# A softmax's division moved from the probabilities to the head's output

## What is computed

```python
q = (layernorm(x) @ wq)          # 32 heads of 128, rotary; scaled by 1/sqrt(128)
k, v = ctx @ wk, ctx @ wv        # 8 heads of 128 over 1024 positions; each serves 4 query heads
attn = softmax(q @ k.T + mask)   # per batch element and head: 512 x 1024
out = attn @ v                   # 512 x 128 per head
x = x + concat(out) @ wo
```

## Time and profile before

| | |
|---|---|
| median of 3 runs | 3843.18 us |
| the runs | 3857.33, 3840.72, 3843.18 us |
| span of the profiled execution (first to last instruction) | 3848.1 us |
| the profiled execution's own time | not listed apart from the runs |
| attention stage in the trace | about 1250 to 2218 us |
| mean granted TensorE clock | 0.905 |

### The profile page before, as it was taken

One profiled execution on the slowest core, in us unless ns is written; L12 is line 12 of the kernel. 1 busy time (PEld: TensorE's weight loads), 2 busy tenths in 40 slices (PEclk: granted clock), 3 DMA queues, 4 the chain that ended last, 5 costly groups with the idle time before them and its releaser, 6 DMA issues. The chain is left out here.

```text
span 3848.1 us, 45676 instructions
## 1 busy us (share of the span) xinstructions
PE 3119.9 (81%) x14144; PEld 2487.0 (65%) x14144; DVE 3251.7 (85%) x4335; ACT 2177.6 (57%) x2742; POOL 1180.3 (31%) x547
## 2 busy tenths in 40 slices
PE   5767665767766999999999977777574699999999
PEld 4555554546645788888888855555442577777787
DVE  7999997877977899999999979999947488878853
ACT  4555554546556677777777655666513265555531
POOL 3777774741732111111111135545100001101000
PEclk8888886889878999999999989989856799999999
DMA  3222223324222211111111032222002212121211
GB/s 107 79 93 71 98 71 103 105 89 142 87 90 93 89 53 52 57 52 54 56 47 58 28 137 98 96 89 87 22 6 88 66 61 77 60 82 61 71 55 52
DMA packets 170336, 286.81 MB, mean 75 GB/s; under 512 B 11712, under 2 KB 98752, under 8 KB 170176
## 3 DMA queue, kind: packets, MB, share of 16 engines
q1 hardware_dynamic: 160960, 268.24, 20.9%
q10 hardware_dynamic: 9216, 16.78, 1.2%
HBM read 196.64 MB, written 88.34 MB: 74 GB/s over the span
## 5 line engine op out<-in xcount | busy, mean ns | idle before, releaser
L220 DVE SCALAR_TENSOR_TENSOR pq_nf_val<-pq_nf_above,pq_nf_val 128x1024 f32<-128x1024 f32 x224 | 449.3, 2006 | 10.2
L898 ACT ACTIVATE at_pth<-at_t 128x512 fp32r<-128x512 f32 x512 | 281.9, 596 | 249.5 <-PE at_t L991 249.5
L205 ACT ACTIVATE pq_nf_above<-pq_nf_raw,sharp 128x1024 f32<-128x1024 f32 x240 | 273.7, 1148 | 256.6 <-DVE pq_nf_val L220 255.1
L220 DVE SCALAR_TENSOR_TENSOR ou_nf_val<-ou_nf_above,ou_nf_val 128x1024 f32<-128x1024 f32 x224 | 395.1, 1764 | 5.8
L205 ACT ACTIVATE ou_nf_above<-ou_nf_raw,sharp 128x1024 f32<-128x1024 f32 x240 | 274.6, 1150 | 197.9 <-DVE ou_nf_val L220 184.3
L117 PE MATMUL pq_pj<-xT_h,pq_wh 128*128 128x512 f32 x512 | 227.4, 444 | 180.1 <-POOL pq_wl L483 180.1
L941 DVE CUSTOM_DVE_ANT_0 at_sc<-at_s,at_mk 128x1024 f32<-128x1024 f32 x256 | 312.1, 1219 | 60.4 <-issue 35.2
L205 ACT ACTIVATE ff_nf_above<-ff_nf_raw,sharp 128x1024 f32<-128x1024 f32 x255 | 291.7, 1148 | 92.4 <-DVE ff_nf_val L220 72.8
L957 DVE TENSOR_TENSOR at_ptl<-at_t,at_pth 128x512 fp32r<-128x512 f32 x512 | 328.0, 682 | 1.1 <-ACT at_pth L898 1.1
L117 PE MATMUL ou_acc<-ou_wh,ou_oh 128*128 128x512 f32 x512 | 225.2, 440 | 127.9 <-DVE X L1158 110.1
L220 DVE SCALAR_TENSOR_TENSOR ff_nf_val<-ff_nf_above,ff_nf_val 128x1024 f32<-128x1024 f32 x238 | 308.0, 1294 | 21.2 <-ACT ff_nf_above L205 18.6
(11 more groups left out here) (210 smaller groups left out, 8710.5 us busy)
## 6 DMA issues: line engine op xcount, KB each, us to landing
ff_raw<-dq SPq DMA_DIRECT2D x63, 512.0 KB, 4.0
pq_raw<-in_L_xattn_wq SPq DMA_DIRECT2D x32, 512.0 KB, 5.0
q_d<-pq_res SPq DMA_DIRECT2D x32, 512.0 KB, 2.6
at_qraw<-q_d SPq DMA_DIRECT2D x64, 256.0 KB, 2.7
o_d<-at_ot ACTq DMA_DIRECT2D x64, 256.0 KB, 2.0
ou_oraw<-o_d SPq DMA_DIRECT2D x32, 512.0 KB, 3.4
ou_wraw<-in_L_xattn_wo SPq DMA_DIRECT2D x32, 512.0 KB, 3.5
pq_nf_raw<-in_L_ffn_w SPq DMA_DIRECT2D x16, 512.0 KB, 5.4
```

The source lines that it names most:

```text
L205: act.activation(self.above[:, (s + j) % 2, 0:width], self.raw[:, s, 0:width], ACT.Relu, bias=self.sharp[:, j:j + 1], scale=SHARP).then_in ...
L220: dve.scalar_tensor_tensor(v, above, STEPS[j], v, ALU.min, ALU.add).then_inc(self.stepped.sem, 1)
L898: act.activation(pt[0][:, h % 2, j * HALF:(j + 1) * HALF, (n % QT) * P:(n % QT + 1) * P], t_ps[:, j], ACT.Copy).then_inc(t_hi.sem, 1)
```

## The change

The probabilities go unnormalised into the transposes and the mix. The division by the row's sum is made on the head's output instead. There a query position is a column and no longer a partition, so the four reciprocals that each partition holds (`inv`, 128 x 4) are stored to DRAM as a row of 512 (`r_d`), and loaded again as that row in every partition (`inv_row`, 128 x 512). GpSimd multiplies the output `ot` by it. Also: the masked score is negated by the masking operation and its minimum taken, so that no separate sign flip is needed (`low` is the bias, scale -1 in the exponential). `turn` waits for `expd` in place of `normed`, `exponentials` for `masked` in place of `maxed`. The store of the head's output moves from ScalarE's queue to SyncE's. SyncE's queue now holds, in the order of steps: loads of `fetches`, `store_inverse` (lag 4), `load_inverse_row` (lag 6), `store_out` (lag 11), with the fetches first in a step.

```diff
-def attention_stage(nc, q_d, k_d, v_d, o_d, mask, ident):
+def attention_stage(nc, q_d, k_d, v_d, r_d, o_d, mask, ident):
...
-        sm = sb("sm", [P, 2, 4], F32)
-        turnstile = sb("turnstile", [P, 1], F32)
+        low = sb("low", [P, 2], F32)
+        sums = sb("sums", [P, 2, QT], F32)
+        inv = sb("inv", [P, 2, QT], F32)
+        inv_row = sb("inv_row", [P, 2, SQ], F32)
+        turnstile = sb("turnstile", [P, 2], F32)
...
+        def passed(b, i, h):
+
+            return i * (16 * HP // 2) + 16 * (b * HQ // 2 + h // 2)
+
...
+        INV_LAG = QT
+        ROW_LAG = QT + 2
...
+            def store_inverse(b, i, h):
+                bb, hh = at(b, i, h)
+                sp.wait_ge(inverted.sem, inverted.done(head(b, i, h)))
+                sp.dma_start(r_d[bb, bass.ds(hh, 1)].rearrange("a (t p) -> p (a t)", p=P),
+                             inv[:, h % 2], allow_slow_non_contiguous=True).then_inc(inv_out[h % 2], 16)
+
+
+            def load_inverse_row(b, i, h):
+                bb, hh = at(b, i, h)
+                sp.wait_ge(inv_out[h % 2], passed(b, i, h) + 32)
+                sp.dma_start(inv_row[:, h % 2], r_d[bb, bass.ds(hh, 1)].broadcast_to((P, SQ))).then_inc(inv_in[h % 2], 16)
+
+            def store_out(b, i, h):
+                bb, hh = at(b, i, h)
+                sp.wait_ge(scaled.sem, scaled.done(head(b, i, h)))
+                sp.dma_start(o_d[bass.ds(hh, 1)].rearrange("a p n -> p (a n)")[:, bb * SQ:(bb + 1) * SQ],
+                             ot[:, h % 2]).then_inc(o_st[h % 2], 16)
+
             def do_step(b, i, n):
                 for kind, x in fetches(b, i, n):
                     fetch(b, i, kind, x)
-
+                for lag, act_on in ((INV_LAG, store_inverse), (ROW_LAG, load_inverse_row), (STORE_LAG, store_out)):
+                    if (n - lag) % QT == 0 and exists(b, i, n - lag):
+                        act_on(b, i, (n - lag) // QT)
...
+            def scale_out(b, i, h):
+                pool.wait_ge(inv_in[h % 2], passed(b, i, h) + 16)
+                pool.wait_ge(copied.sem, copied.done(head(b, i, h)))
+                pool.tensor_tensor(ot[:, h % 2], ot[:, h % 2], inv_row[:, h % 2], ALU.mult).then_inc(scaled.sem, 1)
+
             def do_step(b, i, n):
+                if (n - COPY_LAG) % QT == 0 and exists(b, i, n - COPY_LAG):
+                    scale_out(b, i, (n - COPY_LAG) // QT)
...
             def exponentials(b, i, n):
-                act.wait_ge(maxed.sem, maxed.done(step(b, i, n)))
+                h, quarter = n // QT, n % QT
+                if quarter == 0:
+
+                    act.wait_ge(inverted.sem, inverted.free(head(b, i, h), 2))
+                act.wait_ge(masked.sem, masked.done(step(b, i, n)))
                 act.wait_ge(turned.sem, turned.free(2 * step(b, i, n) + 1, 4))
-                act.activation(pr[:, n % 2], sc[:, n % 2], ACT.Exp, bias=sm[:, n % 2, 1:2],
-                               accum_out=sm[:, n % 2, 2:3]).then_inc(expd.sem, 1)
+                act.activation(pr[:, n % 2], sc[:, n % 2], ACT.Exp, bias=low[:, n % 2:n % 2 + 1], scale=-1.0,
+                               accum_out=sums[:, h % 2, quarter:quarter + 1]).then_inc(expd.sem, 1)
...
-                dve.tensor_tensor_reduce(sc[:, n % 2], s_ps[:, n % 2], mk[:, bb * QT + n % QT], 1.0, NEG,
-                                         ALU.add, ALU.max, sm[:, n % 2, 0:1]).then_inc(masked.sem, 1)
-                dve.wait_ge(masked.sem, masked.done(step(b, i, n)))
-                dve.tensor_scalar(sm[:, n % 2, 1:2], sm[:, n % 2, 0:1], -1.0, None, ALU.mult).then_inc(maxed.sem, 1)
-
-            def normalise(b, i, n):
-                dve.wait_ge(expd.sem, expd.done(step(b, i, n)))
-                dve.reciprocal(sm[:, n % 2, 3:4], sm[:, n % 2, 2:3]).then_inc(recipd.sem, 1)
-                dve.wait_ge(recipd.sem, recipd.done(step(b, i, n)))
-                dve.tensor_scalar(pr[:, n % 2], pr[:, n % 2], sm[:, n % 2, 3:4], None, ALU.mult).then_inc(normed.sem, 1)
+                dve.memset(turnstile[:, n % 2:n % 2 + 1], 0.0)
+                dve.tensor_tensor_reduce(sc[:, n % 2], s_ps[:, n % 2], mk[:, bb * QT + n % QT], -1.0, -NEG,
+                                         ALU.add, ALU.min, low[:, n % 2:n % 2 + 1]).then_inc(masked.sem, 1)
+
+            def invert(b, i, h):
+                dve.wait_ge(expd.sem, expd.done(step(b, i, QT * (h + 1) - 1)))
+                dve.wait_ge(inv_out[h % 2], passed(b, i, h) + 16)
+                dve.reciprocal(inv[:, h % 2], sums[:, h % 2]).then_inc(inverted.sem, 1)
...
-                for lag, act_on in ((0, mask_and_max), (1, normalise), (2, turn_low)):
-                    if exists(b, i, n - lag):
-                        act_on(b, i, n - lag)
+                if exists(b, i, n):
+                    mask_and_min(b, i, n)
+                if (n - INV_LAG) % QT == 0 and exists(b, i, n - INV_LAG):
+                    invert(b, i, (n - INV_LAG) // QT)
+                if exists(b, i, n - 2):
+                    turn_low(b, i, n - 2)
...
-                pe.wait_ge(normed.sem, normed.done(step(b, i, n)))
+                pe.wait_ge(expd.sem, expd.done(step(b, i, n)))
...
+    r_d = scratch("r_d", (B, HQ, SQ))
```

More of the change, by code:

```diff
@@ L754, in attention_stage @@
         o_st = [sem("o_st0"), sem("o_st1")]
+        inv_out = [sem("inv_out0"), sem("inv_out1")]
+        inv_in = [sem("inv_in0"), sem("inv_in1")]
         k_hi, v_hi, q_hi = event("k_hi"), event("v_hi"), event("q_hi")
@@ L759, in attention_stage @@
         masked = event("masked", 2)
-        maxed = event("maxed")
         expd = event("expd", 2)
-        recipd = event("recipd")
-        normed = event("normed")
+        inverted = event("inverted", 2)
+        scaled = event("scaled", 2)
         turned = event("turned", 4)
@@ L835, in do_step @@
                     fetch(b, i, kind, x)
+                for lag, act_on in ((INV_LAG, store_inverse), (ROW_LAG, load_inverse_row), (STORE_LAG, store_out)):
+                    if (n - lag) % QT == 0 and exists(b, i, n - lag):
+                        act_on(b, i, (n - lag) // QT)
+            for s in range(2):
+                sp.sem_inc(o_st[s], 16)
+                sp.sem_inc(inv_out[s], 16)
             for kind, x in FIRST:
@@ L840, in _ @@
             program(sp, do_step)
+            for s in range(2):
+                sp.wait_ge(o_st[s], 16 * (B * HQ // 2 + 1))
         @block.gpsimd
@@ L853, in fetch @@
                     pool.tensor_tensor(qq[1][:, x % 2], qraw[:, x % 2], f32(qq[0][:, x % 2]), ALU.subtract).then_inc(q_lo.sem, 1)
+            def scale_out(b, i, h):
+                pool.wait_ge(inv_in[h % 2], passed(b, i, h) + 16)
+                pool.wait_ge(copied.sem, copied.done(head(b, i, h)))
+                pool.tensor_tensor(ot[:, h % 2], ot[:, h % 2], inv_row[:, h % 2], ALU.mult).then_inc(scaled.sem, 1)
             def do_step(b, i, n):
+                if (n - COPY_LAG) % QT == 0 and exists(b, i, n - COPY_LAG):
+                    scale_out(b, i, (n - COPY_LAG) // QT)
                 for kind, x in fetches(b, i, n):
                     fetch(b, i, kind, x)
+            scaled.open(pool)
             k_lo.open(pool)
@@ L904, in copy_out @@
                 act.activation(ot[:, h % 2], o_ps[:, h % 2], ACT.Copy).then_inc(copied.sem, 1)
[L906 to L910, removed]
             def do_step(b, i, n):
@@ L918, in do_step @@
                     exponentials(b, i, n)
-                for lag, act_on in ((COPY_LAG, copy_out), (STORE_LAG, store_out)):
-                    if (n - lag) % QT == 0 and exists(b, i, n - lag):
-                        act_on(b, i, (n - lag) // QT)
+                if (n - COPY_LAG) % QT == 0 and exists(b, i, n - COPY_LAG):
+                    copy_out(b, i, (n - COPY_LAG) // QT)
             expd.open(act)
             copied.open(act)
-            for s in range(2):
-                act.sem_inc(o_st[s], 16)
             for kind, x in FIRST:
@@ L929, in _, with mask_and_min @@
             program(act, do_step)
-            for s in range(2):
-                act.wait_ge(o_st[s], 16 * (B * HQ // 2 + 1))
         @block.vector
         def _(dve):
-            def mask_and_max(b, i, n):
+            def mask_and_min(b, i, n):
                 bb = at(b, i, n // QT)[0]
@@ L938, in mask_and_max @@
                 dve.wait_ge(expd.sem, expd.free(step(b, i, n), 2))
-                dve.memset(turnstile[:], 0.0)
-                dve.tensor_tensor_reduce(sc[:, n % 2], s_ps[:, n % 2], mk[:, bb * QT + n % QT], 1.0, NEG,
-                                         ALU.add, ALU.max, sm[:, n % 2, 0:1]).then_inc(masked.sem, 1)
-                dve.wait_ge(masked.sem, masked.done(step(b, i, n)))
-                dve.tensor_scalar(sm[:, n % 2, 1:2], sm[:, n % 2, 0:1], -1.0, None, ALU.mult).then_inc(maxed.sem, 1)
-            def normalise(b, i, n):
-                dve.wait_ge(expd.sem, expd.done(step(b, i, n)))
```

(13 more changed lines are left out.)

## The result

| | before | after |
|---|---|---|
| median | 3846.89 us (4 runs) | 4467.32 us (4 runs) |
| ratio to before, 95% interval | | 1.1612 (1.1583 to 1.1641) |
| span of the profiled execution | 3848.1 us | 4462.8 us |
| mean granted clock | 0.905 | 0.857 |

The account below looks back on a forecast made before the run. TensorE was taken to bound the attention stage, with VectorE waiting for it. The late Q's +108 us, less 21 of gains, plus 1.4 for the last multiply, gave +88: 3931 us on the median, range 3838 to 3990.

Parts of the forecast that it names:

- The bound: Attention stage: TensorE sets the 3.61 us step, so the 1.05 us of VectorE given up per step gains nothing directly.
- The gains: K and V fetches lose their excess, 19 us, and four loop boundaries give 2 us: 21 us in all.
- GpSimd's multiply, the row load, the masked minimum: Multiply 1.28 us, hidden except +1.4 us after the last head; row load hidden; masked minimum costs nothing.
- SyncE's queue: Q load stands behind the store that waits for the reciprocal: store out at R + 0.16, Q load at R + 0.68.
- The latest time for Q: Q must land by R + 3.4 us, which it just does if the store adds no delay.
- The store's price: 512 elements of 4 bytes ahead of Q's packets: delay 0 to 4.0 us, taken as 1.74, 62 times, 108 us.
- the middle one: Store's packets at the parameter loads' rate, 234 a us: 2.26 us for 528, delaying Q by 1.74 us.
- Both rows that it rested on: Packet rates for the store: 256-byte packets at 966 a us, and 4-byte parameter loads at 234 a us.
- the rule on small transfers: Skill's rule that transfers under 512 B are read-modify-write; the trace was said to agree, 234 against 966 packets a us.
- The third rival: Store much slower than the parameter loads, above 3.3 us: from +147 us, 4071 us at 4.5; chance 0.10.
- K and V: K load late behind the output's store: 1.6 us, 15 times, 24 us, hidden by a late Q; V costs nothing.
- The base of the sum: Profiled execution taken as the 3857.3 us run, giving 3945 us; the median of 3843.2 gives the forecast 3931.

Follow-up runs that it names:

- the last version: New kernel with loads issued far ahead and the inverse stored as 128 elements of 16 bytes, read by GpSimd at that stride: 3828.3 us, ratio 0.9935.
- the spread store: New kernel with the 512 4-byte elements stored 256 bytes apart and the row loaded from other data: 3880.34 us, ratio 1.0065.
- The fill run: New kernel with five extra float32 matmuls, results unread, ahead of the transposes that wait for the late Q: 4474.29 us, ratio 1.1614.

## Why the prediction was wrong

The direction was right; 4467 us lies far above the range of 3838 to 3990.

*The bound.* Right. The median step is 3.61 us before, without the division and in the last version, and a microsecond less of VectorE per step did not shorten it. The gains were put at 21 us and measured at 26.5; the first steps, left out of the sum, may be the rest.

*GpSimd's multiply, the row load, the masked minimum.* Right: 1.28 us and hidden; the row load lands in 4.6 us and is not waited for.

*SyncE's queue.* The mechanism was right, with its times: store at R + 0.20 and Q's load at R + 0.81 (0.16 and 0.68 forecast; R is the end of the reciprocal). The latest time for Q was right too. In the trace with elements 256 bytes apart, where the clock stays at 1.00, a head's period (from the end of one reciprocal to the end of the next) can be cut at the start of Q's cast. Over the 62 heads the first part is 3.7 us or more, and the rest is 11.03 us in the median (11.10 in the mean). A head takes 4 x 3.614 = 14.46 us without a wait, so Q may be cast up to 3.43 us after R without cost.

*The store's price: the step that failed.* "What delays it is the store itself", and there "I take the middle one": 2.26 us of packets, a delay of 1.74, 108 us in all, with 4.5 us as the upper bound. Both rows that it rested on told how fast packets start, and by both the store's would have started more slowly than they did (0.55 and 2.26 us forecast, all 528 within 0.4 us measured). The row of the parameter loads, was misread besides. The DMA engines were busy for a tenth of that window (the last number below), so that 234 packets a us was no rate at which they were full. The store's 528 started at over 1300 a us:

```profile
q1 hardware_dynamic: 327, 0.00, 10.5%
```

What counts is what follows the start of the packets: the store lands after 9.9 us, and Q is cast 11.76 us after R (mean of the 62), 8.33 us too late: 62 x 8.33 = **516 us** in place of 108. Twice a row of small loads from DRAM was no bound for small writes into it. With that row fall the 1.74 us of the sum, the 4.5 us of the bound, and the reading that the trace agrees with the rule on small transfers. The third rival had the right direction and the wrong size, and got a chance of 0.10.

*The two statements of the Trainium skill.* "DMA: Bandwidth & Descriptors", section "Specifications", has read-modify-write under 512 B. It pointed the right way (9.9 us here), though no run shows a read-modify-write as such, and the size alone doesn't decide: with 64 bytes between them elements of 4 bytes land in 2.2 us. The 10.5 ns a packet of its section "Bandwidth" agrees with how fast the packets start here (33 on an engine within 0.4 us, an estimated 12 ns each). It says nothing of when they have landed, and taken for the store's whole price it pointed the wrong way.

*Missing from the sum: the clock.* The rest of a head's period is 13.10 us on average in the new kernel, 11.10 with the spread store. 62 x 2.0 = **124 us**. That it is the clock, the steps show: added up, the 61 steps behind a wait are 135 us over 3.61 each, and in each of them the granted clock accounts for the excess. The fill run shows it too, by the 16 heads in which the clock stayed up. A granted clock of 1.00 in the earlier trace rows was the clock of an engine that never waits; I carried it to one that waits once a head.

*The sum.* 516 + 124 - 26.5 (the gains of the version without division) + 1.4 = 615 us, against 620 measured. The first two terms are taken from the trace itself, so the sum shows that nothing large is left out and is no second proof of the causes.

*K and V.* As forecast: ScalarE waits 14.9 us for K in all, and the late Q hides it. K shows once Q is on time, by 102.8 us in the run with Q's load first and by 35 in the one with elements 256 bytes apart (24 forecast). V lands after 13.5 us and is hardly waited for (5.8 us in all).

*The base of the sum.* That only the run of 3857.3 us could contain the span of 3848.1 was misread: a run's time is 1.8 us above its span (4464.58 and 4462.8 after). That gives some 3850 us for the profiled run. The forecast of 3931 stood on the median and is not touched.

*Still open:* why Q is late by some 5 us in some heads and by some 10 in others (8.7 to 14.4 us after R, often two and two in turn); why Q is slow beside a store on the other queue in one head of three; and what the memory does with 4-byte neighbours.

## What to carry to other kernels

Before a small transfer is added to a queue, ask what stands behind it and when that is needed; here the whole loss came from one in-order queue, and the same transfer cost nothing measurable once the loads were issued ahead of its waits. Store a column of 4-byte scalars so that one partition's values lie side by side (16 bytes here), or 64 bytes apart, and undo the order in the reader's access pattern. When an engine at full clock is going to wait several microseconds, price the slow clock after the wait as well as the wait. And before a row of the trace is used as a rate, ask whether the engine was busy in it; twice a rate from another direction of transfer is no bound.

## What the runs showed of the hardware that I had not expected

- 512 writes of 4 bytes into one 2 KB row of DRAM take 9.9 us to land; the same 64 or 256 bytes apart 2.2 and 2.1; 16 bytes apart 3.0; 128 of 16 bytes side by side 1.4. The packets of the slowest are all started within 0.4 us.
- The slow store holds the loads behind it on its own queue (Q 11.8 us in the median, never under 8.0). Beside it on the other queue Q took 2.5 to 3.7 us in 43 heads and 4.3 to 11.5 in 19, against 2.5 to 3.5 in the kernel before.
- A store of 256 KB issued while the row load of 256 KB was on its way took 4.3 us in the median, 2.0 when alone. With the slow store issued behind it too, it took 5.3 us and up to 15.5.
- After 4.8 to 11.2 us of idleness TensorE did a step at a mean granted clock of 0.53 to 0.73 in place of 1.00, between the levels of 1.2 and 2.4 GHz, and the step took 4.98 to 6.54 us in place of 3.61. After the 1.73 us that the fill left in one head it took 3.84.
- GpSimd's multiply of 128x512 takes 1.56 us in place of 1.28 when one input has a stride of 16 bytes.
